# One-hots built by 128- and 159-column comparisons with scalars, smaller index tables, and reordered work in cross-attention

## The reference, cut to what matters

```python
x = x + tanh(g_xattn[0]) * L0_xattn(layernorm(x), ctx, ctx)        # window 64, 16 heads
x = x + tanh(g_ffn[0])   * L0_ffn(layernorm(x), ...)               # top 8 of 32, groups
x = x + tanh(g_xattn[1]) * L1_xattn(layernorm(x), ctx, ...)        # similarity, softmax both ways
x = x + tanh(g_ffn[1])   * L1_ffn(layernorm(x), ...)               # top 2 of 8, biased choice
...
logits = flat @ gate_w.T
scores = sigmoid(logits)
topk_w, topk_i = _group_topk(scores)
...
# of each chosen expert: silu(x @ wg.T) * (x @ wu.T) @ wd.T, weighted and summed over the choices
```

## Time and profile before

| | |
|---|---|
| time, median of 3 executions | 1096.98 us (1096.69 to 1097.93) |
| profiled execution | 1101.13 us, span 1099.3 us |
| TensorE busy | 930.9 us (85%), mean granted clock 0.921 |
| VectorE busy | 694.2 us (63%), 2,004 instructions |
| ScalarE busy | 440.9 us (40%) |
| GpSimd busy | 539.9 us (49%) |
| token table L810 on the chain of waits | 3% of the span |

### The profile page before, as it was taken

One profiled execution on the slowest core, in us unless ns is written; L12 is line 12 of the kernel. 1 busy time (PEld: TensorE's weight loads), 2 busy tenths in 40 slices (PEclk: granted clock), 3 DMA queues, 4 the chain that ended last, 5 costly groups with the idle time before them and its releaser, 6 DMA issues.

```text
span 1099.3 us, 20610 instructions
## 1 busy us (share of the span) xinstructions
PE 930.9 (85%) x5516; PEld 713.5 (65%) x5517; DVE 694.2 (63%) x2004; ACT 440.9 (40%) x1030; POOL 539.9 (49%) x575
## 2 busy tenths in 40 slices
PE   3458888887699999999999917979999998999893
PEld 2357777776545888888888504645656564787672
DVE  5669999997674865555555247765868246443334
ACT  4548888893052444444444302122222313232220
POOL 7246665644004755555653577875700000786651
PEclk9679999998757999999999967979999998999997
DMA  8960000003101776777768737342300011466647
GB/s 243 216 128 2 1 0 0 0 1 105 46 1 47 224 221 202 224 217 218 211 198 139 282 97 275 102 140 88 112 11 20 1 52 29 87 111 116 143 83 244
DMA packets 75225, 127.44 MB, mean 116 GB/s; under 512 B 12480, under 2 KB 52032, under 8 KB 75008
## 3 DMA queue, kind: packets, MB, share of 16 engines
q0 software_dynamic: 21264, 48.02, 19.2%
q1 hardware_dynamic: 32240, 57.47, 17.2%
q10 hardware_dynamic: 21632, 20.85, 5.4%
HBM read 80.62 MB, written 36.77 MB: 107 GB/s over the span
## 4 chain that ended last, share of the span: by engine, by line
PE 58%; DVE 19%; DMA 7%; issue 7%; POOL 5%; ACT 2%; SPq 2%; DVEq 0%; ACTq 0%; POOLq 0%
PE bank L914 17%; PE bank L929 9%; PE bank L1600 5%; DVE ptl L618 4%; PE bank L903 4%; DMA sw<-in_w 3%; PE bank L810 3%; POOL yg L1193 3%; PE bank L1500 3%; PE bank L424 2%; DVE nmax L610 2%; PE bank L922 2%; PE bank L1535 2%; PE bank L1657 2%; PE bank L1560 2%
## 5 line engine op out<-in xcount | busy, mean ns | idle before, releaser
L1178 POOL DMA_INDIRECT xg<-token_rows,gather_idx x198 | 190.1, 960 | 314.2 <-DMA token_rows<-cw 134.3
L914 PE MATMUL bank<-sw,xgt 128*128 x948 | 244.9, 381 | 0.5 <-issue 0.5
L914 PEld LDWEIGHTS bank<-sw,xgt 128*128 128x128 f32 x948 | 165.4, 191 | 15.5 <-issue 0.8
L1193 POOL DMA_INDIRECT yg<-slot_rows,slot_of x128 | 139.0, 1086 | 67.3 <-issue 34.1
L1007 ACT ACTIVATE ssil<-bank 128x128 f32<-128x128 f32 x237 | 65.7, 278 | 199.9 <-PE bank L914 199.9
L929 PE MATMUL bank<-sw,sht 128*128 x474 | 144.8, 388 | 0.0
L1099 DVE COPY xgt<-bank 128x256 f32<-128x256 f32 x198 | 83.8, 424 | 85.0 <-PE bank L903 75.2
L1112 DVE COPY sht<-bank 128x128 f32<-128x128 f32 x237 | 69.0, 291 | 105.9 <-PE bank L922 105.5
L546 ACT ACTIVATE prob<-bank,nmax 128x256 f32<-128x256 f32 x256 | 111.7, 511 | 8.0 <-DVE nmax L610 8.0
L424 PE MATMUL bank<-consts,prob 128*128 128x128 f32 x512 | 82.6, 285 | 37.3 <-DVE ptl L618 35.0
L610 DVE TENSOR_REDUCE nmax<-bank 128x2 f32<-128x512 f32 x128 | 87.6, 685 | 17.7 <-PE bank L411 17.2
(11 more groups left out here) (218 smaller groups left out, 1648.6 us busy)
## 6 DMA issues: line engine op xcount, KB each, us to landing
slot_rows<-ysb ACTq DMA_DIRECT2D x79, 256.0 KB, 3.3
sw<-in_w SPq DMA_DIRECT2D x48, 384.0 KB, 3.6
kst<-khl SPq DMA_DIRECT2D x32, 224.0 KB, 6.0
token_sums<-zeros SPq DMA_DIRECT2D x2, 2176.0 KB, 12.2
token_rows<-xn SPq DMA_DIRECT2D x8, 512.0 KB, 3.9
sums<-token_sums SPq DMA_DIRECT2D x8, 512.0 KB, 7.2
xg<-token_rows,gather_idx POOLq DMA_INDIRECT x198, 3.5
x<-in_x SPq DMA_DIRECT2D x4, 512.0 KB, 6.8
```

The costliest lines, as they stand in the source:

```text
L914: mm = pe.matmul(bank[2 + k % 2][:, 0:2 * FF], xgt[:, i % 3, c * P:(c + 1) * P], w[:, :, c, :], start=(c == 0), stop=(c == CH - 1))
L1178: nc.gpsimd.indirect_dma_start(xg[:, (first + i) % XG_RING, 0:ROW[L]], None, rows[L], bass.IndirectOffsetOnAxis(gather_idx[:, i:i + 1], 0) ...
L1193: nc.gpsimd.indirect_dma_start(yg[:, t % Y_TILES, j, :], None, ybuf[L], bass.IndirectOffsetOnAxis(slot_of[:, t, j:j + 1], 0)).then_inc(s_y ...
```

## The change

The one-hots are written one choice at a time, contiguously: 8 pairs of comparisons for a tile of layer 0 and 2 for one of layer 1, each of an index table of 128 or 159 (39) columns with one column of posl or posh as a scalar for each partition. The comparison for hot_tok multiplies by token_id in the same instruction, so ScalarE's part and its semaphore go. posl and posh are kept in 32 bits. The index tables hold each index once. ScalarE makes a one-column Silu behind the Sigmoid. In cross-attention three idle products stand between the transposes and the scores of batches 0 and 1, the first pair of additions of the next batch stands ahead of the first shared_hidden, and the inverse roots of attention in batch 3 and of the feed-forward in batches 2 and 3 are made by GpSimd behind its gathers.

```diff
+        iota_lo = sb("iota_lo", [P, P], F16)
+        iota_col = sb("iota_col", [P, BLOCKS[0]], F16)
...
+        posl = sb("posl", [P, TILES, 8], F32, rt)
+        posh = sb("posh", [P, TILES, 8], F32, rt)
+        hot_tok = sb("hot_tok", [P, HOTS, 8, P], F16, rt)
+        hot_hi = sb("hot_hi", [P, HOTS, 8, BLOCKS[0] + 1], F16, rt)
...
-                pe.wait_ge(m.hots, m.n["hots"] + t + 1)
+                pe.wait_ge(m.hot, m.n["hot"] + t + 1)
                 for j in range(top):
-                    mm = pe.matmul(bank[5][:, P:P + cols], hot_tok[:, t % HOTS, :, j], hot_hi[:, t % HOTS, 0:cols, j],
+                    mm = pe.matmul(bank[5][:, P:P + cols], hot_tok[:, t % HOTS, j, :], hot_hi[:, t % HOTS, j, 0:cols],
...
-            hots_by_token(act, 0, m, range(TILES))
+            act.wait_ge(m.lgl, 1)
+            nc.scalar.activation(unread[:, :], tg[:, 0:1], ACT.Silu)
...
-                nc.gpsimd.iota(iota_lo[:, :, :], [[1, P], [0, 8]], base=0, channel_multiplier=0,
+                nc.gpsimd.iota(iota_lo[:, :], [[1, P]], base=0, channel_multiplier=0,
                                allow_small_or_imprecise_dtypes=True)
-                nc.gpsimd.iota(iota_col[:, :, :], [[1, BLOCKS[0]], [0, 8]], base=0, channel_multiplier=0,
+                nc.gpsimd.iota(iota_col[:, :], [[1, BLOCKS[0]]], base=0, channel_multiplier=0,
...
-                nc.vector.tensor_tensor(hot_lo[:, t % HOTS, :, 0:top], iota_lo[:, :, 0:top],
-                                        posl[:, t:t + 1, 0:top].broadcast_to([P, P, top]), ALU.is_equal)
-                op = nc.vector.tensor_tensor(hot_hi[:, t % HOTS, 0:cols, 0:top], iota_col[:, 0:cols, 0:top],
-                                             posh[:, t:t + 1, 0:top].broadcast_to([P, cols, top]), ALU.is_equal)
+                for j in range(top):
+                    nc.vector.tensor_scalar(hot_tok[:, t % HOTS, j, :], iota_lo[:, :], posl[:, t, j:j + 1],
+                                            token_id[:, t:t + 1], ALU.is_equal, ALU.mult)
+                    op = nc.vector.tensor_scalar(hot_hi[:, t % HOTS, j, 0:cols], iota_col[:, 0:cols],
+                                                 posh[:, t, j:j + 1], None, ALU.is_equal)
                 op.then_inc(m.hot, 1)
...
                 transposes(b)
+                if b < 2:
+                    kept_busy(pe, bank[7], 3)
...
                     logits_taken(b - 1)
+                if b + 1 < BATCH:
+                    y_pair_added(dve, 0, 4 * b + 4)
+                if b:
                     shared_hidden(b - 1, 0)
                 largest(b)
                 negated_maximum(b)
-                if b + 1 < BATCH:
-                    y_pair_added(dve, 0, 4 * b + 4)
                 products(b)
...
+            ln_rsqrt(pool, 2, 3, was=3)
+            ln_rsqrt(pool, 3, 2, was=2)
+            ln_rsqrt(pool, 3, 3, was=2)
```

More of the change, by code:

```diff
@@ L124, in gated_xattn_moe_kernel @@
         rbias = sb("rbias", [P, E1], F32)
-        iota_lo = band_f32[:, 2 * DIM:4 * DIM].bitcast(F16).rearrange("p (a j) -> p a j", j=8)
-        iota_col = sb("iota_col", [P, BLOCKS[0], 8], F16)
+        iota_lo = sb("iota_lo", [P, P], F16)
+        iota_col = sb("iota_col", [P, BLOCKS[0]], F16)
+        unread = sb("unread", [P, 1], F32)
         token_id = sb("token_id", [P, TILES], F32)
@@ L236, in gated_xattn_moe_kernel @@
         s_ln = [sem(f"ln_stats{i}") for i in range(4)]
-        s_lnp = [sem(f"ln_rsqrt{i}") for i in range(2)]
+        s_lnp = [sem(f"ln_rsqrt{i}") for i in range(4)]
         s_root = sem("ln_root_step")
@@ L281, in gated_xattn_moe_kernel @@
             "hot": 16,
-            "hots": 16,
             "hotf": 15,
@@ L316, in __init__ @@
                 self.hot = own["hot"]
-                self.hots = own["hots"]
                 self.hotf = own["hotf"]
@@ L734, in ln_stats, with ln_rsqrt @@
             op.then_inc(s_ln[n], 1)
-        def ln_rsqrt(pool, n, b):
+        def ln_rsqrt(pool, n, b, was=0):
             ts = slice(TPB * b, TPB * b + TPB)
@@ L739, in ln_rsqrt @@
             nc.gpsimd.tensor_scalar(varp[:, ts], meanvar[:, ts, 1], EPS, None, ALU.add).then_inc(s_lnp[n], 1)
-            pool.wait_ge(s_lnp[n], 2 * b + 1)
+            pool.wait_ge(s_lnp[n], 2 * (b - was) + 1)
             nc.gpsimd.tensor_tensor(rstd[:, ts], varp[:, ts], minus_half[:, :], ALU.pow).then_inc(s_lnp[n], 1)
@@ L963, in sparse_tensor @@
             down(blocks * halves - 1)
[L965 to L972, removed]
         def front0_scalar(act, m):
@@ L1146, in tables @@
                 pool.wait_ge(s_tabs, 1)
-                nc.gpsimd.tensor_scalar(before[:, :], iota_lo[:, :, 0], part_id[:, 0:1], None,
+                nc.gpsimd.tensor_scalar(before[:, :], iota_lo[:, :], part_id[:, 0:1], None,
                                         ALU.is_gt).then_inc(s_tabs, 1)
@@ L1339, in gather_lists @@
             link(nc.vector.tensor_reduce(incl[0:ne, :], diag[0:ne, 0:ne], AX_X, ALU.add))
-            nc.vector.tensor_scalar(started[0:ne, 0:cols], iota_col[0:ne, 0:cols, 0], incl[0:ne, 0:1], None,
+            nc.vector.tensor_scalar(started[0:ne, 0:cols], iota_col[0:ne, 0:cols], incl[0:ne, 0:1], None,
                                     ALU.is_ge).then_inc(m.bexp, 1)
@@ L1724, in scalar_a1 @@
                 shared_silu(b, u)
-            hots_by_token(act, 1, m, range(TILES))
         def vector_a1(dve, root, m, first, routing, tables):
@@ L1814, in attended_normalised @@
                 ln_stats(dve, 3, b)
-                dve.wait_ge(s_ln[3], 2 * b + 2)
-                ln_root(root, b)
+                if b >= 2:
+                    dve.wait_ge(s_lnp[3], 2 * (b - 1))
+                else:
+                    dve.wait_ge(s_ln[3], 2 * b + 2)
+                    ln_root(root, b)
                 ln_norm(dve, 3, b, m.xn)
@@ L1879, in vector_a1 @@
                     stats_of_summed(dve, b + 1)
-                    dve.wait_ge(s_ln[2], 2 * b + 4)
-                    ln_root(root, b + 1)
+                    if b + 1 == BATCH - 1:
+                        dve.wait_ge(s_lnp[2], 2)
+                    else:
+                        dve.wait_ge(s_ln[2], 2 * b + 4)
+                        ln_root(root, b + 1)
                     ln_norm(dve, 2, b + 1, A["xn"])
```

## The result

The changed kernel takes 1113.17 us (median; 1111.15 to 1117.98), the kernel before 1096.84 beside it: a ratio of 1.0147 (95% interval 1.0108 to 1.0186), so it is slower by some 16 us. The forecast of 1103.7 had the direction and, at the upper end of its range, the time; its size was less than half of what came.

What follows compares the result with a forecast made beforehand. No engine bounds throughout; in layer 0's routing TensorE's token table does, and VectorE would become the bound. 13.3 + 3.8 − 7.1 − 1.3 − 2 = +6.7 us on 1096.98 gave 1103.7 us, range 1092 to 1115.

Steps and rivals of the forecast that it cites:

- The one-hots, +13.3 and +3.8: Routing of layers 0 and 1: short VectorE comparisons, 0.40 us a pair in layer 0, lengthen the stretches by 13.3 and 3.8 us.
- 0.06 us for each scalar from memory: VectorE's one-hot comparisons: each scalar read from memory adds some 0.06 us to an instruction's fixed cost.
- the doubled rate of 16-bit columns: VectorE's one-hot comparisons: 16 bits halve the column cost to 0.26 ns, so 0.03 and 0.04 us per comparison.
- the free scalars: Rival on VectorE's one-hots: scalars from memory cost nothing when instructions follow closely; pair 0.22 us, kernel 1076 us; chance 0.15.
- the 16-bit columns no faster than 32-bit ones: Rival on VectorE's one-hots: 16 bits bring no column speedup; pair 0.48 us, kernel 1115 us; chance 0.13.
- The tail of 1.7 us: Layer 0's token table: TensorE's work remaining after VectorE's last comparison, at most 2.3 us, taken as 1.7.
- The small index tables, −7.1: Layer 0 before routing: shorter GpSimd tables free VectorE, remove TensorE's 3.13 us wait and keep its clock up: −7.1 us.
- with no wait I expect both at the full level: Layer 0's last transposes and 32 router products run at full clock: −0.9 and −3.1 us of the −7.1.
- the clock at 270 falls all the same: Rival on layer 0's router products: TensorE's clock still drops; −3.1 in place of −7.1, kernel 1108 us; chance 0.12.
- The early Silu, −1.3: First expert: loading ScalarE's function table behind the Sigmoid takes 1.28 us off the chain: −1.3 us, 0 if something reloads.
- The idle products, −2: Cross-attention, batch 1: idle products fit TensorE's 1.86 us wait and hold its clock for the scores: −2, between 0 and −3.
- Additions and roots, 0: Additions moved into VectorE's waits: 0, or +0.8 where cover falls short; three roots moved to GpSimd: 0, to −1.

Runs made afterwards that it cites:

- the constants: Changed kernel with constants in place of posl, token_id and posh in layer 0's comparisons, so the table is empty: ratio 1.0664.
- the one-hots alone: Changed kernel without early Silu, idle products, moved additions and moved roots; new one-hots and small index tables stay: ratios 1.0117 and, measured again, 1.0106.
- tables held back: Kernel before, with GpSimd's index tables made to wait until VectorE's last normalisation of layer 0 is done: ratio 0.9940.
- TensorE kept at work: Changed kernel with five more idle products ahead of layer 0's first router transposes: ratio 1.0117, 1112.89 us.
- the other parts alone: Kernel before plus early Silu, three idle products, moved additions and moved roots; one-hots and index tables as before: ratio 1.0000.
- pairs with idle products: Kernel before with choices interleaved by two, GpSimd's tables delayed behind the last normalisation, and idle products before router transposes and scores: ratio 0.9805, 1079.05 us.
- pairs: Kernel before with its long comparisons, but choices interleaved by two instead of eight and smaller index tables: ratio 0.9879, 1082.81 us.
- pairs with tables held back: Kernel before with choices interleaved by two and GpSimd's index tables delayed until after the last normalisation: ratio 0.9826.

## Why the prediction was right in direction and short in size

**The one-hots, +13.3 and +3.8: right.** Measured +12.3 and +3.5 (layer 1: 12.3 to 15.8 us from its first comparison to gather_idx). The pair cost 0.39 us against a forecast of 0.40. The step that carried it, 0.06 us for each scalar from memory, is shown by the constants: with them 0.10 and 0.11 us, with two and one scalars from memory 0.22 and 0.17. So is the doubled rate of 16-bit columns: 0.19 + 0.03 and 0.14 + 0.04 fit, the 32-bit slope doesn't. Two rivals fall by this, the free scalars and the 16-bit columns no faster than 32-bit ones. The Trainium skill's 75 ns ("Vector Engine (DVE) Microarchitecture Reference", "Measured stream behaviour on trn2") holds for constants (0.10 less 0.03) and is short by 0.06 us for each scalar from memory. The tail of 1.7 us was 1.4.

**The small index tables, −7.1: the step that failed as a sure gain.** The first half, that VectorE is freed and TensorE's wait of 3.13 us goes, is shown: the wait is gone, or down to 0.83 us, in every profile with these tables. The second, "with no wait I expect both at the full level", held in three of the six profiles of kernels with these tables and no added idle products before the router. In five of the six the clock falls already in or right behind an *earlier* wait, the 2.9 us before the first transposes. In three of them (the changed kernel's third, both of the one-hots alone) it is back for the third batch, and the stretch takes 6.3 us. In two (the changed kernel's first and second) it stays low through all router products, which costs as much as the gain or more. In the sixth, the one with constants, it holds through the earlier wait; then a wait of 0.83 us is left, the clock falls within the last products, and the stretch takes 8.98.

The step had a gap that the profile of the kernel before hid. There TensorE's first 16 transposes ran at the low level, behind the same earlier wait:

```profile
260.15 3.52 PE L776 MATMUL bank<-consts,xn 128*128 128x128 f32 x16 [2.89 <-DVE xn L760]
```

That made TensorE late, so its earlier products ended just when VectorE would be done, at about 268. Where the clock held through these transposes, with the tables held back, TensorE came to the third batch's router products 1.1 us earlier, measured from the start of the last normalisations, and a wait was left. In no profile did TensorE both hold the full level from the first transposes on and find no wait before the last ones.

The rival "the clock at 270 falls all the same" named the right place for the profile with constants, at a change of −4.8 where it had −3.1. For the changed kernel's first two it had the wrong place, and its price of 4 us was too low: over the three profiles of the changed kernel the stretch changed by −0.05, +0.77 and −7.47, −2.2 on the mean. The third profile excludes that the parts outside the one-hots force the low clock. Whether they make it likelier, three profiles against two can't tell, and what decides it between executions stays open.

**The early Silu, −1.3: wrong.** The load is gone from the chain, and the next gather is late instead, at the same time: the 41st Silu comes 73.7 to 74.2 us behind gather_idx in the five profiles with the early one and the layer 0 gathers intact, and 73.9 to 74.1 in the two of the one-hots alone, the kernel before and the tables held back. The prediction priced what stood on the chain and didn't ask what stood right behind it.

**The idle products, −2: mis-sized.** With them the scores of batches 0 and 1 take 7.2 to 7.8 us in all profiles, close to the full level's 7.24. But the 10.19 us that the prediction read for batch 1 are not what it always takes without them:

```profile
720.08 7.32 PE L1489 MATMUL bank<-craw,aenc 128*128 128x512 f32 x16 [1.86 <-issue]
```

This is batch 1 in the second profile of the one-hots alone, which has no idle products there; the wait of 1.86 us is the same, and the clock held. With the tables held back it took 7.32 as well. From the first gather of layer 0's outputs to layer 1's mask, six profiles with the idle products (the three of the changed kernel, TensorE kept at work, the other parts alone, the pairs with idle products) have a mean of 294.4 us, six with neither (before, one-hots alone twice, tables held back, pairs, pairs with tables held back) 295.3. The difference, 0.9, is smaller than the spread within either six, 3 and 5 us, so the runs don't tell it from nothing.

**Additions and roots, 0: not contradicted.** Together with Silu and idle products they change nothing, 1.0000 (0.9975 to 1.0026); no run has them alone.

Put together, as an estimate from these profiles: +12.3 + 3.5 − 2.2 − 0.9 + 0 = +12.7 us, where the three measurements of the changed kernel give ratios of 1.0147, 1.0120 and 1.0099, or +16, +13 and +11 on some 1,097. Against this estimate the predicted +6.7 was too hopeful by 6 us, 4.9 of it in the index tables and 2.4 in Silu and idle products, less 1.3 for the one-hots. The −2.2 is the softest term: it is a mean of three profiles with two outcomes some 7.5 us apart, and over all six profiles with these tables and no added idle products before the router it would be −4.4.

One profile's total says little about such a term, because stretches that no edit is meant to touch differ as much between executions. The last normalisations of layer 0 start between 261.89 and 266.58 us, and from layer 1's gather_idx to the end all profiles but the one with constants take 169.0 to 175.2 us; the kernel before has the shortest of these, 169.0. That may be why five added idle products restored most of the stretch in a profile and not the median; it is not shown.

**What the change was after can be had otherwise.** The costly part of the old table was a moving operand with 16 bytes between its columns. Contiguous one-hots cure that (0.07 to 0.13 us a product), but 256 short instructions on VectorE cost more than that gains. Interleaving by two cures it as well, with VectorE's 32 long instructions left as they were: −16 us in the same stretch. The Trainium skill ("SBUF — State Buffer", "Specifications (TRN2)") has 16-byte lines that want at least two hits each for full bandwidth; with one hit to a line the runs show 0.28 us a product, with four 0.13 or 0.076.

## What to carry to other kernels

Price an instruction by its start-to-start time with the same kind of operands: here two scalars from memory cost four times as much as the 128 columns that they were compared with. When one engine reads badly laid-out data, look for the mildest layout that suits the reader before splitting the writer's instructions; here a step of 4 bytes (0.076 us a product) was nearly as good as none (0.069). And a gain that hangs on TensorE's clock is not to be booked in full from one profile: look at each wait ahead of it, and at more than one execution. Ask too whether an engine was late in that profile only because its clock had been low; once it is not, the wait that you took away can come back.

## What the hardware showed unasked

- ScalarE writing 16-bit results 256 bytes apart needs 5.04 us for 1,024 columns, against 1.15 us with neighbours side by side.
- TensorE's product of 159 columns does not care about the layout of its weights (0.282 us with contiguous, 0.288 with interleaved ones), but strongly about that of its moving operand. With 16 bytes between columns it takes 0.286 us at the low clock level and 0.288 at the full one in the kernel before; contiguous, 0.133 at the low level and 0.069 at the full one.
- GpSimd's index tables cost little by their columns: 128 groups of 8 equal entries take 1.94 us, 128 groups of 2 take 1.53, and a single run of 128 entries takes 0.24.
- Executions of one program can run the same 32 router products in 3.66 or in 6.87 us.
